# VectorE's cosine multiply reads PSUM, in two halves placed around the scaling of keys; raw projections in one shared buffer

## The reference, cut to what matters

```python
x = x + attention_0(layernorm(x))           # 16 heads of 8
x = x + layers(layernorm(x))                # six layers, below: the change is here
x = x + attention_1(layernorm(x))
x = x + moe(layernorm(x))                   # 16 experts

def attn_layer(x, Wqkv, qs, ksc, Wo):       # 16 heads of 64, windows of 32
    q, k, v = split(x @ Wqkv)
    q = l2norm(q) * qs
    k = l2norm(k) * ksc
    q = q * cos * scale + rotate_half(q) * sin * scale
    k = k * cos / scale + rotate_half(k) * sin / scale
    out = local_attention(q, k, v)          # each window sees itself and the one before
    return out @ Wo
for i in range(6):
    x = attn_layer(shift_tokens(x), ...) + x
    x = ffn_layer(shift_tokens(x), ...) + x # layer norm, 128 -> 2 x 341, gelu gate, -> 128
```

## Time and profile before

| what | us |
|---|---|
| median of 3 runs | 2728.71 (2722.62 to 2735.03) |
| the profiled execution, its own time | 2730.72 |
| its span | 2728.9 |
| busy in the span: PE, DVE, ACT, POOL | 2169.6 (80%), 1973.4 (72%), 1509.5 (55%), 1492.2 (55%) |
| loads of TensorE weights (beside the matmuls) | 1154.6 (42%) |
| the slots of the six layers, from the first L602 to the last | 432.2 to 2147.6 |

### The profile page before, as it was taken

How to read it: one execution, slowest core, us unless ns; L and a number is a source line. 1 busy time by engine, 2 the same in 40 slices (tenths; PEclk the granted TensorE clock), 3 DMA queues, 4 the chain that set the end, 5 groups by cost and what they waited for, 6 DMA issues and landing times.

```text
span 2728.9 us, 53797 instructions
## 1 busy us (share of the span) xinstructions
PE 2169.6 (80%) x21684; PEld 1154.6 (42%) x21780; DVE 1973.4 (72%) x2087; ACT 1509.5 (55%) x1863; POOL 1492.2 (55%) x1031
## 2 busy tenths in 40 slices
PE   4768875888998989888889889889988756678734
PEld 1111123555555555555555555555555411111334
DVE  1766628888888888888888888888889426676211
ACT  2255564566676666666766676666766321455600
POOL 5500017777776776777776777777777234100033
PEclk7787897999999999999999999999999866897967
DMA  4100000000001000100010000000000001000133
GB/s 149 60 19 25 13 2 1 17 2 17 2 2 26 17 2 2 26 2 17 1 26 2 17 2 9 19 17 2 1 9 2 1 18 67 22 27 13 32 92 86
DMA packets 55828, 59.08 MB, mean 22 GB/s; under 512 B 13142, under 2 KB 45012, under 8 KB 55508
## 3 DMA queue, kind: packets, MB, share of 16 engines
q1 hardware_dynamic: 53444, 50.77, 6.1%
q0 software_dynamic: 2128, 4.72, 0.7%
HBM read 44.07 MB, written 11.01 MB: 20 GB/s over the span
## 4 chain that ended last, share of the span: by engine, by line
PE 36%; POOL 19%; DVE 17%; issue 16%; ACT 9%; DMA 2%; SPq 1%; POOLq 0%; DVEq 0%; ACTq 0%
PE bank L735 5%; PE bank L706 4%; PE bank L859 4%; DVE big L1463 4%; PE bank L923 4%; PE bank L933 4%; POOL big L580 3%; POOL big L597 3%; POOL big L581 3%; DVE big L1569 3%; POOL small L590 2%; ACT big L1180 2%; ACT pxs L1305 2%; PE bank L976 2%; DVE small L1563 2%
## 5 line engine op out<-in xcount | busy, mean ns | idle before, releaser
L1463 DVE TENSOR_REDUCE big<-bank 128x1 f32<-128x512 f32 x512 | 327.7, 685 | 199.3 <-PE bank L706 195.3
L602 POOL TENSOR_TENSOR sc<-sc,small 128x1024 f32<-128x1024 f32 x96 | 263.4, 2744 | 365.4 <-DVE small L1605 365.4
L859 PE MATMUL bank<-wqk,xs 128*128 128x512 f32 x768 | 359.2, 610 | 13.6 <-ACT xs L1261 8.3
L933 PE MATMUL bank<-pxs,mw 128*128 128x256 f32 x1536 | 366.2, 382 | 0.0
L1296 ACT ACTIVATE sc<-sc 128x1024 f32<-128x1024 f32 x96 | 101.5, 1057 | 464.0 <-DVE sc L1595 463.9
L933 PEld LDWEIGHTS bank<-pxs,mw 128*128 128x128 f32 x1536 | 291.1, 192 | 102.7 <-issue 71.9
L1180 ACT ACTIVATE big<-bank 128x1024 f32<-128x1024 f32 x256 | 250.2, 1026 | 140.1 <-PE bank L720 137.1
L1569 DVE TENSOR_TENSOR big<-big,rotCl 128x2048 f32<-128x2048 f32 x96 | 226.2, 2356 | 78.1 <-POOL big L581 78.1
L706 PE MATMUL bank<-pxs 48*128 48x512 bf16 x512 | 183.6, 439 | 117.1 <-DVE big L1463 74.0
L1563 DVE TENSOR_REDUCE small<-big 128x32 f32<-128x2048 f32 x96 | 219.0, 2281 | 39.5 <-ACT big L1274 30.2
L1584 DVE TENSOR_TENSOR big<-big,small 128x1024 f32<-128x1024 f32 x192 | 246.5, 1284 | 1.1 <-POOL small L592 1.1
(11 more groups left out here) (244 smaller groups left out, 3945.1 us busy)
## 6 DMA issues: line engine op xcount, KB each, us to landing
wqk<-in_L_ffn_Wqkv SPq DMA_DIRECT2D x12, 512.0 KB, 4.4
pxs<-part_rows SPq DMA_DIRECT2D x64, 96.0 KB
pxs<-part_rows SPq DMA_DIRECT2D x64, 64.0 KB
wqk<-in_L_ffn_w SPq DMA_DIRECT2D x16, 256.0 KB, 3.0
wvt<-in_wv_layers_t SPq DMA_DIRECT2D x6, 512.0 KB, 4.7
wol<-in_L_ffn_Wo SPq DMA_DIRECT2D x6, 512.0 KB, 5.8
part_rows<-big SPq DMA_DIRECT2D x24, 128.0 KB
part_rows<-sc SPq DMA_DIRECT2D x24, 128.0 KB
```

What stands on the lines that cost most here:

```text
L602: pool.tensor_tensor(p3, p3, rden(i).unsqueeze(2).broadcast_to([P, LH, 64]), ALU.mult).then_inc(l_pn, 1)
L859: m = pe.matmul(bank[:, 2 - 2 * half + c, :], xs[:, b % 2, WIN + i * P:WIN + (i + 1) * P], wqk[:, (2 * half + c) * 512:(2 * half + c + 1) ...
L933: m = pe.matmul(bank[:, 6, part * 2 * P:(part + 1) * 2 * P], mw[:, 2 * (a % 4) + s, a // 4, :], pxs[:, part, a, s, :], start=(a == 0 and s ...
L1463: dve.tensor_reduce(nm[:, qt, 2 * p + r:2 * p + r + 1], bank[:, 4 + r, :], AX.X, ALU.max, negate=True).then_inc(a_mx, 1)
```

## The change

Raw projections go to one new buffer `rw` that all tiles share, so ScalarE's `take` of a tile has to wait until GpSimd's `turn_swapped` of the tile before has read it (and its squares have been taken). VectorE's plain turn no longer works in place: each half reads the projection from PSUM and writes `raws(i)`. It is done for T+2 rather than T+1: half 0 behind `sums` of T, then the scaling of keys of T+1, then half 1, and only after these the feed-forward pieces at the end of the slot. `l_ra` now counts two per tile. Wherever TensorE waited for `l_raw` before it overwrites the banks, it also waits for `l_ra`.

```diff
--- before.py
+++ after.py
@@ -147,6 +147,7 @@
         v2 = vbuf[:, :].rearrange("p (b w t) -> p b w t", b=2, w=4)
         big = sb("big", [P, 4, 2048])
         rotB, sq = big[:, 2, :], big[:, 3, :]
+        rw = sb("rw", [P, 2048])
         sc = sb("sc", [P, 4, 1024])
         mask_f = sc[:, 0, 0:768]
         small = sb("small", [P, 8, 32])
@@ -573,7 +574,7 @@
                 if not (isinstance(T, int) and T == 0):
                     pool.wait_ge(l_aq, T)
                     pool.wait_ge(l_ak, T)
-                q4 = raws(i).rearrange("p (a h d) -> p a h d", a=2, h=LH)
+                q4 = rw[:, :].rearrange("p (a h d) -> p a h d", a=2, h=LH)
                 r4 = rotB.rearrange("p (a h d) -> p a h d", a=2, h=LH)
                 tab = rotSl[:, i, :].rearrange("p (a d) -> p a d", a=2).unsqueeze(2).broadcast_to([P, 2, LH, LD])
                 h = LD // 2
@@ -592,7 +593,7 @@
                 pool.tensor_tensor(y, y, u, ALU.mult).then_inc(l_nr, 1)
 
             def add_keys(T, i):
-                pool.wait_ge(l_ra, T + 1)
+                pool.wait_ge(l_ra, 2 * T + 2)
                 pool.wait_ge(l_rb, 2 * T + 2)
                 pool.tensor_tensor(raws(i)[:, INNER:], raws(i)[:, INNER:], rotB[:, INNER:], ALU.add).then_inc(l_ak, 1)
 
@@ -863,6 +864,7 @@
             def turn_keys(T, i, ahead):
                 if ahead >= 1:
                     pe.wait_ge(l_raw, 2 * T + 4)
+                    pe.wait_ge(l_ra, 2 * T + 4)
                 else:
                     pe.wait_ge(l_kd, T)
                 pe.wait_ge(l_yk, T + 1)
@@ -874,6 +876,7 @@
             def turn_queries(T, l, b, i):
                 if isinstance(T, int) and T < 2:
                     pe.wait_ge(l_raw, 2 * T + 3)
+                    pe.wait_ge(l_ra, 2 * T + 3)
                 else:
                     pe.wait_ge(l_pc, 2 * T - 2)
                 if b == 0 and i == 3:
@@ -1039,6 +1042,7 @@
                     pe.wait_ge(l_e, T + 1)
                     if ahead >= 2:
                         pe.wait_ge(l_raw, 2 * T + 5)
+                        pe.wait_ge(l_ra, 2 * T + 5)
                     else:
                         pe.wait_ge(l_qe, T + 1)
                     settle(pe)
@@ -1056,6 +1060,7 @@
                 for half in range(2):
                     if T == 1:
                         pe.wait_ge(l_raw, 1 + half)
+                        pe.wait_ge(l_ra, 1 + half)
                     project(0, 0, 0, T, half)
             layer_slots(pe, slot)
             N = DEPTH * BATCH * TILES
@@ -1263,7 +1268,11 @@
             def take(T, i, half):
 
                 act.wait_ge(l_qk, 2 * T + half + 1)
-                act.activation(raws(i)[:, half * INNER:(half + 1) * INNER],
+                if half == 0 and not (isinstance(T, int) and T == 0):
+                    act.wait_ge(l_rb, 2 * T)
+                    act.wait_ge(l_sq, T)
+                    settle(act)
+                act.activation(rw[:, half * INNER:(half + 1) * INNER],
                                bank[:, 2 - 2 * half:4 - 2 * half, :].rearrange("p a t -> p (a t)"), ACT.Copy).then_inc(l_raw, 1)
 
             def squares(T, i):
@@ -1271,7 +1280,7 @@
                 if not (isinstance(T, int) and T == 0):
                     act.wait_ge(l_ss, T)
                 settle(act)
-                act.activation(sq, raws(i), ACT.Square).then_inc(l_sq, 1)
+                act.activation(sq, rw[:, :], ACT.Square).then_inc(l_sq, 1)
 
             def guess(T, i):
 
@@ -1563,14 +1572,17 @@
                 ch.link(dve.tensor_reduce(ss, sq.rearrange("p (h d) -> p h d", d=LD), AX.X, ALU.add))
                 dve.tensor_scalar(ss, ss, 1e-24, -0.5, ALU.max, ALU.mult).then_inc(l_ss, 1)
 
-            def turn_plain(T, i):
+            def turn_plain(T, i, half):
+                dve.wait_ge(l_raw, 2 * T + half + 1)
+                src = bank[:, 2 - 2 * half:4 - 2 * half, :].rearrange("p a (h d) -> p (a h) d", d=LD)
+                tab = rotCl[:, i, half * LD:(half + 1) * LD].unsqueeze(1).broadcast_to([P, LH, LD])
+                dve.tensor_tensor(raws(i)[:, half * INNER:(half + 1) * INNER].rearrange("p (h d) -> p h d", d=LD), src, tab,
+                                  ALU.mult).then_inc(l_ra, 1)
+
+            def add_queries(T, i):
+                dve.wait_ge(l_ra, 2 * T + 1)
                 dve.wait_ge(l_rb, 2 * T + 2)
-                r4 = raws(i).rearrange("p (a h d) -> p a h d", a=2, h=LH)
-                dve.tensor_tensor(r4, r4, rotCl[:, i % TILES, :].rearrange("p (a d) -> p a d", a=2).unsqueeze(2).broadcast_to([P, 2, LH, LD]),
-                                  ALU.mult).then_inc(l_ra, 1)
-
-            def add_queries(T, i):
-                dve.wait_ge(l_ra, T + 1)
+                settle(dve)
                 dve.tensor_tensor(raws(i)[:, 0:INNER], raws(i)[:, 0:INNER], rotB[:, 0:INNER], ALU.add).then_inc(l_aq, 1)
 
             def scaled(T, i, half):
@@ -1666,7 +1678,6 @@
                 if not (first and i == 0):
                     turn_probs(T - 1, (i - 1) % 2)
                 if ahead >= 1:
-                    turn_plain(T + 1, (i + 1) % TILES)
                     add_queries(T + 1, (i + 1) % 2)
                 if b == BATCH - 1 and i == 2 and more:
                     tables(l + 1)
@@ -1680,8 +1691,12 @@
                 if i == 3 and not first:
                     centre(it - 1)
                 sums(T, i)
+                if ahead >= 2:
+                    turn_plain(T + 2, (i + 2) % TILES, 0)
                 if ahead >= 1:
                     scaled(T + 1, (i + 1) % 2, 1)
+                if ahead >= 2:
+                    turn_plain(T + 2, (i + 2) % TILES, 1)
                 if i == 1 and feeds:
                     hidden(it - 2, 0)
                     hidden(it - 2, 1)
@@ -1692,8 +1707,10 @@
 
             dve.wait_ge(step_done, LAYER0 + 1)
             tables(0)
+            for T in range(2):
+                for half in range(2):
+                    turn_plain(T, T, half)
             square_sums(0, 0)
-            turn_plain(0, 0)
             add_queries(0, 0)
             scaled(0, 0, 0)
             scaled(0, 0, 1)
```

2 lines of the change are left out of this document (1 added, 1 removed).

## The result

Over four runs each on one chip the changed kernel took 2823.25 us (2819.8 to 2829.68) and the kernel before 2731.87 (2722.62 to 2738.51): a ratio of 1.033, 95% interval 1.0305 to 1.036, slower. The profiled execution took 2829.68 us, its span is 2827.9, which is 99 us more than the 2728.9 of before. The forecast was 2825 (range 2750 to 2885), 96 us over the 2728.71 that was the kernel before's median when the forecast was made.

What follows compares the result with a forecast made beforehand. With VectorE and TensorE near 90% busy, the order inside one slot was taken to decide. Terms 49.5+32-6+12-4.5+24-7-8+4 summed to +96 us over the median of 2728.71, giving 2825 us, range 2750 to 2885 (own range 2770 to 2870).

Steps and rivals of the forecast that it cites:

- What VectorE gets: VectorE's slot: the 1.18 us wait for GpSimd goes and the row maximum could start at R+10.3 instead of R+11.4.
- the first rival: TensorE's order has slack and VectorE alone ends each slot, so 1.1 us a slot is gained: 2626 us; chance 0.08.
- What TensorE gets: `weigh` on TensorE must also wait for half 0 of tile T+2 and can start no earlier than R+1.45.
- Into i=1: 22 slots with the gated layer: distance between reciprocals (R to R) 19.15 us instead of 16.91, +2.25 each, 49.5 us.
- The clock: TensorE idles 3.3 us before `weigh` in i=0, then runs at half clock: 1.8 us more in 8 of 10 slots, 32 us.
- Into i=2: 22 slots: scores end and VectorE arrive together, -0.2 each, -6 us with table slots; the next `weigh` starts about R+2.8.
- Into i=3: Late `weigh` makes the distance 18.2 against 17.07: 12 us over 11 slots; five behind the table slots gain 4.5 us.
- Slots where scores already ended last: First batch of a layer into i=3 and loop's head into i=0, five each: the whole delay passes, 24 us.
- The plain slots: Plain slots of the first two batches: -1.1 us in 7, together -8 us.
- both cancel: Rival: `weigh`'s delay is half absorbed and the clock holds, +18 us or less, about 2740; chance 0.08.
- The half clock: Rival: gaps of 1 to 2 us before `weigh` bring half clock in other slots too, 2890 us; chance 0.08.
- a half from PSUM is held like one from SBUF: Rival: GpSimd holds half 0, which ends 1.9 us later, and `weigh` with it, in 57 slots: 2933 us; chance 0.04.

Runs made afterwards that it cites:

- the kernel with TensorE kept busy: The changed kernel with three added matmuls of 512 columns on TensorE in i=0, between mixing and `weigh`, output unread: 2802.75 us, ratio 1.027.
- the wait alone: The kernel before with one wait added: `weigh` of T-1 also waits for VectorE's scaled keys of T+1: 2839.36 us, ratio 1.038.

## Why the prediction was right

**What VectorE gets** held step by step, as the slot of R = 1331.85 shows. Into i=0 the distance fell by 0.99 in 12 slots; there VectorE sets the pace, as the first rival had it for all slots. In the five that enter a layer's second batch it rose by 0.80 where 0.2 was forecast.

**What TensorE gets** held: R+1.44 for R+1.45. **Into i=1** came out at +2.34 each for +2.25. The chain named, through ScalarE's gate and gelus, is one of two that end together; without the gelus the slot is still 18.79. In the trace after, the eviction starts at R+3.5 plus what the prolonged `weigh` adds, and the exponentials wait for nothing in 17 of 24 slots, as forecast.

**The clock** was over-sized: 17 to 19 us by two ways (the sum of distances, and the kernel with TensorE kept busy) against 32. The 3.3 us of idle I had worked out was 2.5 to 2.95, and `weigh` was prolonged in 12 of 23 slots, not in 8 of 10.

**Into i=2**: the ordinary slots gave -0.19 as forecast, but by scores that ended last, not by both arriving together: moving `hidden(0)` took off another 0.95. The step failed where I counted the table slots among the others. They fell by 2.6 each, 13 us together, where the forecast had 6 us for all 22. Two table products of VectorE with both inputs in SBUF (L1623 before, L1635 after) take 0.85 us together instead of 2.95. From one such slot, before (R = 659.62) and after (R = 677.81):

```profile
672.54 2.95 DVE L1623 TENSOR_TENSOR rotSl<-rotS,qks 128x256 f32<-128x256 f32 x2
672.69 2.52 POOL L597 TENSOR_TENSOR big<-big 128x1024 f32<-128x1024 f32 x1
...
690.22 0.85 DVE L1635 TENSOR_TENSOR rotSl<-rotS,qks 128x256 f32<-128x256 f32 x2
690.75 2.53 POOL L598 TENSOR_TENSOR big<-big 128x1024 f32<-128x1024 f32 x1
```

Before, GpSimd's addition of keys started first and the second product lasted until it was done (675.49 for 675.21); after, the second product had started 0.15 ahead of the addition.

**Into i=3** (+14.3 for +12) and the lateness of TensorE at R+2.68 (for 2.8) held; that it comes from `hidden(0)` behind both halves is borne out by the wait alone, where these slots lose 0.3, but not by moving `hidden(0)` in the changed kernel, which left them as they were.

**Slots where scores already ended last** were under-sized, 33 for 24. Of these the first batches' slots into i=3 grew by some 4.7 us each, not 2.8. In the slot behind R = 1077.10:

```profile
1085.39 1.97 PE L872 MATMUL bank<-ident,big 128*128 128x128 f32 x8
...
1093.76 0.31 PE L905 MATMUL bank<-kbuf,qT 64*32 64x64 f32 x6 [1.48 <-issue]
```

Eight transposes take 1.97 instead of 1.09, and a pause of 1.2 to 1.8 us, called "issue", stands in the middle of the scores. Both are in all five slots after; of the five in the kernel before one has the slow transposes and none the pause. Without the gelus the transposes take 1.09, the pause stays, and the slots grow by 2.9. What makes the pause is open.

**The plain slots** gave nothing where I had -8 (-1.1 in 7). Three of the seven fell by 1.0 to 1.2 as forecast, one stayed, and three grew: 1.2 (in the table with the middle batches), 1.8, and 5.1 in the first layer's first batch into i=3, which belongs to the kind above. The last slot of all fell by 3.3. **The rest**: the start cost 5.9 for 4, and 2.4 came behind the last R; as the start also differs by up to 11 us between kernels whose start is the same, neither is shown to be the change's. Errors of -15, -10, +9, +8 and +4 us cancelled; that 2825 came within 2 us of 2823.25 is luck, the terms do not deserve it. The forecast's own range was also mis-added: with its terms "no clock loss, half of the 24" gives 2825-32-12 = 2781, not 2770.

**The rivals.** That TensorE's order has slack was refuted by the two kernels that add only a wait: it has about 1.2 us behind i=0, not 3.5. That both cancel was refuted by the +96. The half clock did not come in every slot: behind i=1, 2 and 3 `weigh` was prolonged in 2 of 72 cases, once behind 3.61 us of idle and once behind 1.97; the others had 0 to 1.96. That a half from PSUM is held like one from SBUF was refuted: 1.17 and 1.21 in the timeline, while L603 works beside the first, and 1192 ns mean over 192; the same multiply from SBUF went to 3.33. The Trainium skill, page "SBUF — State Buffer", section "Who interferes with whom", says that a VectorE instruction with two SBUF inputs contends with a GpSimd instruction that reads SBUF, and that one with at most one does not, outside the modes that use both ports; the trace agrees for these multiplies. My own rule, "where VectorE has two SBUF inputs", was too narrow: the tiny tensor_scalar that I read as held by GpSimd (0.84 in the earlier trace rows) has one SBUF input, and after the change it lasts 0.18 in 45 slots and some 1.2 in most others.

**The fixed price of PSUM.** The forecast gave 0.19 us for two halves over one whole as an estimate from the table of the Trainium skill, page "VectorE: DVE Perf Modes", section "The TRN2 errata", and left it out of the sum. The two pages show 1192 ns twice against 2356 once, 0.03 more, but that mean mixes multiplies that stood behind a wait (mostly 2.45) with 29 that did not, 27 of which took 2.24 or 2.25. Against these the halves, 1.17 and 1.21 by their medians, are 0.14 longer, near the estimate. From start to the next start they are not: 1.09 and 1.13 against 2.28, where the next operation needs the result. So no run here settles the price.

What stays open: why the profile calls `weigh`'s wait "issue" after the change and VectorE in the kernel with the wait alone; what makes the pause in the scores of the first batches; and two buffers for the raw values, which were not tried.

## What to carry to other kernels

A producer's bank in PSUM comes free when its last reader is done. Before a second engine is made to read it, find who refills the bank, what stands behind that instruction in its queue, and how much slack it has at the moment the new reader ends; here 1.2 us of slack met 3.5 us of delay, and the kernel lost 1 us a slot. The same edit for the one half whose bank nobody is waiting for gained 0.6 a slot.
